# First group of a Mamba-2 kernel: GpSimd splits projection weights two pairs ahead

## Chip, cores and metric

The kernel runs on one core of a Trainium2 chip. The metric is the time on the device, in microseconds, as the median of several executions.

## The reference, cut

The input `x` is (2, 256, 512) in float32. Three blocks follow one another; the first, a Mamba-2 layer, takes nearly all of the time and is the one that the change touches.

```python
h = layernorm(x); h = rms(h) * norm_w
proj = h @ in_proj_w.T                       # gate 8192, hidden 8192, B 1024, C 1024, dt 128
hBC = silu(causal_conv(hBC, conv_w, conv_b)) # 4 taps
dt = softplus(dt + dt_bias);  A = -exp(A_log)
L = exp(segsum(A * dt))                      # decay between two positions, 0 above the diagonal
y = ((C @ B.T) * L) @ (hid * dt) + Dp * hid  # 128 heads of 64; B and C shared by 16 heads
y = y * silu(gate);  y = group_rms(y, 8 groups) * gnorm_w
x = x + (x_of_layer + y @ out_proj_w.T)
x = x + fake_quant(layernorm(x)) @ fake_quant(ctx)        # second block
x = x + ffn(layernorm(x))                                 # third block, with a small mixture
```

## The kernel before

**Tiling.** The 128 heads are worked as 64 pairs of 128 channels, all 512 tokens at once; eight pairs make a group (one group of the norm, one B and one C). Loops run over pairs: a *slot* `k` of group `g` does the front half of pair `s = 8g + k` and the back half of the pairs before it. `slots` writes the eight slots of the first group out, then a hardware loop over groups 1 to 6, then the last group. Each engine runs its own program in this slot order, and semaphores alone join them, so the order within an engine is what the code says and an instruction that waits holds up all that stand behind it on its engine.

**Precision.** Every large product is made in three passes, with each operand split into an upper part and a rest: `w_hi*h_hi + w_hi*h_lo + w_lo*h_hi`. The split of the weights is GpSimd's work. For a pair it makes `win_hi` and `win_lo` (`split_in`, `lower_in`: 128x1024, the projections to hidden and gate) from `w_raw`, and `wout_hi` and `wout_lo` (`split_out`, `lower_out`: 128x512, the output projection). `win_*` have two buffers, so the split of pair `p` may start only when TensorE has projected the gate of pair `p - 2` (semaphore `pe_gate`). `w_raw` has four buffers, filled by SyncE's queue, and a buffer is free when `lower_out` has read it (`low_wout`).

**A slot on each engine (pair s):**

- SyncE loads the weights (`w_raw`) and the rows of cumulated decay of the pair, broadcast to 128 partitions (`csx`), the latter once ScalarE is through with the pair two before (`act_exp`).
- GpSimd, for the next pair: `own_sums` (a tiny copy, `cs_own`), the split, and `select`, which fills the part above the diagonal in `csx` (two instructions). Then `sum_squares`, and the split of the output weights of this pair. In slot 4 it also splits the B and C weights of the next group (`wbc_hi`, `wbc_lo`, `lower_bc`).
- ScalarE: `decays` (8 exponentials from `csx`, and a table load before them), `tap` (first tap of the convolution, out of `ps_h`), `upper_y`, `square`, a table load, `hidden` and `gates` (two SiLUs). `decays` stands first, from slot 4 on, so all of it waits for `select`.
- VectorE: `combine` (`v`, `yg`), `scale_hidden`, `mask` (decay times C·B, 128x1536), three taps of convolution, `lower_y`.
- TensorE: hidden projection (`ps_h`), gate projection (`ps_z`), output projection of pair s - 3 (`ps_out`), the scan products of pair s - 1 (`ps_y`), and `turn`, four transposes of `hidT`, which need ScalarE's `hidden` of this slot.

TensorE, ScalarE and VectorE each have code of their own for slots 0 to 3 of the first group; GpSimd had it for slots 0 to 2. The small constants of the second block (`constants`, twelve instructions on VectorE) are made in slot 0.

Of the kernel before, what the change touches and what calls it, by code (L numbers as in the profile page):

```python
# [14 lines left out]
PPG = PAIRS // GROUPS  # L15
# [27 lines left out]
def build(nc, x_d, ctx_d, wdt_d, dtpar_d, normw_d, wmain_d, wpar_d, wbc_d, quant_d, wffn_d, ffnb_d,  # L43
# [5 lines left out]
    with ExitStack() as ctx:  # L49
# [170 lines left out]
        def _(eng):  # L220
# [15 lines left out]

            def slot(eng, s, g, k, first, last):
                r = k % 4
                if not (first and k < 4):

                    if late(s - 7):
                        eng.wait_ge(dve_ylo, s - 7)
                    eng.dma_start(par[:, k, :], wpar_d[s]).then_inc(w_in[r], 16)
                    if late(s - 3):
                        eng.wait_ge(low_wout, s - 3)
                    eng.dma_start(w_raw[:, r, :], wmain_d[s]).then_inc(w_in[r], 16)
                if first and k == 1:

                    eng.wait_ge(pre_pe, PE_TOK)
# [34 lines left out]
        def _(eng):  # L284
# [67 lines left out]
            def slot(eng, s, g, k, first, last):  # L352
# [12 lines left out]
                if first and k == 1:  # L365
                    eng.wait_ge(act_exp, 1)
                    own_sums(2, 0)
                    eng.wait_ge(w_in[3], 32)
                    eng.wait_ge(pe_gate, 2)
                    split_in(3, 1)  # L370
                    lower_in(3, 1, 4)
                    eng.wait_ge(csx_in[0], 64)
                    select(0)
                    split_out(1)
                    lower_out(1, 2)
                    return
                if first and k == 2:
                    eng.wait_ge(act_exp, 2)
                    own_sums(3, 1)
                    eng.wait_ge(csx_in[1], 64)  # L380
                    select(1)
                    split_out(2)
                    lower_out(2, 3)
                    return
                if k == 3 and not first:
                    eng.wait_ge(pe_out, s - 3)
                    eng.wait_ge(dve_ms, g)
                    eng.tensor_tensor(rstd[:], ms[:], half_neg[:], ALU.pow).then_inc(pool_rstd, 1)
# [13 lines left out]

                if not (last and k == PPG - 1):
                    split_in(n4, (k + 1) % 2)
                    if first:
                        lower_in(n4, (k + 1) % 2, s + 2)
                        eng.wait_ge(csx_in[1 - r2], 32 * (4 * g + (k + 1) // 2 + 1))
                    else:
                        eng.wait_ge(csx_in[1 - r2], 32 * (4 * g + (k + 1) // 2 + 1))
                        lower_in(n4, (k + 1) % 2, s + 2)  # L410
                    select(1 - r2)
                if k != 3 and late(s - 3):
                    eng.wait_ge(pe_out, s - 3)
# [338 lines left out]
        def _(eng):  # L752
# [87 lines left out]
            def slot(eng, s, g, k, first, last):  # L840
                if first and k == 0:
                    conv_hidden(0, 0)
                    conv_group(1, 0, ps_y, gate[:, 1, :])
                    conv_hidden(1, 1)
                    for b, bank in ((1, ps_out[:, 2, :]), (0, ps_out[:, 3, :])):
                        eng.wait_ge(pe_cb, 2 - b)
                        eng.tensor_copy(cbm[:, b, :], bank[:, 0:MJ]).then_inc(dve_cb, 1)
                    constants()
                    return
                if first and k == 1:  # L850
                    scale_hidden(1, 1)
# [10 lines left out]
                if first and k == 3:  # L862
                    combine(3, 3)
                    scale_hidden(3, 3)
                    mask(3, 0, 3)
                    lower_y(3, 3)
                    return
                combine(s, k)
                scale_hidden(s, k)
# [321 lines left out]
        def _(eng):  # L1191
# [157 lines left out]
            def project_out(s, g, k, tiles=range(TT)):  # L1349

                pair, q2, q4 = (k - 3) % PPG, (k - 3) % 2, (k - 3) % 4
                eng.wait_ge(dve_ylo, s - 2)
                for t in tiles:
                    if k == 3 and late(TT * g):
# [297 lines left out]
```

## Time and profile before

| what | us |
|---|---|
| median of 3 executions | 791.51 (788.96 to 791.81) |
| the profiled execution, its own time | 791.84 |
| its span in the profile | 789.7 |
| TensorE busy | 774.6 |
| GpSimd busy | 696.3 |
| VectorE busy | 636.4 |
| ScalarE busy | 596.5 |

The span is what the profile covers; the execution's time has about 2.1 us around it. Busy times overlap: TensorE at 98% of the span leaves some 15 us in which it does nothing, and the question for any change here is which of these stand in the stretch that it touches (the first group lies between about 20 and 120 us). Times in microseconds in the timelines are counted from the span's start.

### The profile page before, as it was taken

What the parts mean: (1) busy time and instruction counts of PE and PEld (TensorE: products, weight loads), DVE (VectorE), ACT (ScalarE), POOL (GpSimd) and SP (SyncE); (2) the same over time, 40 slices, a digit from 0 to 9 for tenths busy, and PEclk for the clock granted to TensorE, in tenths of its full rate; (3) what the DMA queues carried; (4) which work ended last, traced back from release to release, by engine and by line L of the source; (5) the groups of instructions that cost most, each with busy time, mean ns of one, the idle gap of its engine ahead of it and who ended that gap; (6) DMA issues with size and microseconds to landing.
All of it is one profiled execution on the core that took longest, in us unless ns stands there. A gap on an engine that the chain in (4) does not pass through costs nothing.

```text
span 789.7 us, 13488 instructions
## 1 busy us (share of the span) xinstructions
PE 774.6 (98%) x4275; PEld 611.2 (77%) x4275; DVE 636.4 (81%) x753; ACT 596.5 (76%) x1055; POOL 696.3 (88%) x553
## 2 busy tenths in 40 slices
PE   8989899999999999999999999999999999999997
PEld 7767677877887777877787777877787778877765
DVE  6888787888879886889779886888778778798875
ACT  5799677788778877788678877787687877788552
POOL 6689999899889998899889998999899998899551
PEclk9999999999999999999999999999999999999999
DMA  8356243344254433444243324434343333431001
GB/s 327 119 159 209 91 135 101 128 135 133 67 160 133 133 111 115 133 131 127 74 160 127 116 99 131 135 113 129 109 133 116 122 123 100 136 114 66 1 2 54
DMA packets 58028, 94.94 MB, mean 120 GB/s; under 512 B 13168, under 2 KB 46064, under 8 KB 58000
## 3 DMA queue, kind: packets, MB, share of 16 engines
q1 hardware_dynamic: 57712, 94.06, 37.6%
q10 hardware_dynamic: 288, 0.52, 0.2%
q8 instruction: 15, 0.25, 0.1%
q14 instruction: 13, 0.11, 0.0%
HBM read 93.26 MB, written 1.31 MB: 120 GB/s over the span
## 4 chain that ended last, share of the span: by engine, by line
PE 90%; POOL 4%; DVE 3%; ACT 2%; issue 1%; DMA 0%; DVEq 0%; POOLq 0%; ACTq 0%
PE ps_z L1222 25%; PE ps_out L1357 21%; PE ps_h L1222 21%; PE ps_y L1344 11%; PE ps_t L1195 4%; POOL win_lo L305 1%; PE ps_out L1195 1%; PE ps_t L1367 1%; DVE conv L814 1%; DMA acc<-in_x 0%; POOL csx L343 0%; POOL wout_lo L310 0%; POOL win_hi L296 0%; PE ps_h L1330 0%; PE ps_t L1330 0%
## 5 line engine op out<-in xcount | busy, mean ns | idle before, releaser
L305 POOL TENSOR_TENSOR win_lo<-w_raw,win_hi 128x1024 fp32r<-128x1024 f32 x64 | 182.0, 2843 | 9.7 <-DMA csx<-cs_rows 4.7
L604 ACT ACTIVATE decay<-csx,cs_own 128x256 f32<-128x256 f32 (+1 forms) x512 | 184.4, 443 | 0.8
L814 DVE SCALAR_TENSOR_TENSOR conv<-ps_h,par,conv 128x510 f32<-128x510 f32 (+2 forms) x192 | 142.9, 744 | 20.0 <-ACT conv L533 15.4
L604 ACT ACT_TABLE_LOAD x63 | 80.8, 1283 | 90.0 <-PE ps_y L1344 82.0
L899 DVE TENSOR_TENSOR decay<-decay,cbm 128x1536 f32<-128x1536 f32 x64 | 145.5, 2273 | 0.3 <-ACT decay L604 0.3
L343 POOL TENSOR_SCALAR_AFFINE_SELECT csx<-csx 128x512 f32<-128x512 f32 x128 | 109.3, 877 | 2.5 <-DMA csx<-cs_rows 2.5
L958 DVE SCALAR_TENSOR_TENSOR v<-hidT,par,ps_y 128x512 f32<-128x512 f32 x64 | 47.8, 747 | 78.3 <-PE ps_y L1344 78.2
L1357 PE MATMUL ps_out<-wout_hi,y_hi 128*128 128x512 f32 x252 | 100.3, 398 | 0.0
L1344 PE MATMUL ps_y<-decay,hid_dt 128*64 128x256 f32 (+1 forms) x1024 | 97.3, 332 | 2.4 <-DVE decay L899 1.3
L1357 PE MATMUL ps_out<-wout_lo,y_hi 128*128 128x512 f32 x252 | 99.6, 395 | 0.0
L1357 PE MATMUL ps_out<-wout_hi,y_lo 128*128 128x512 f32 x252 | 99.3, 394 | 0.0
L310 POOL TENSOR_TENSOR wout_lo<-w_raw,wout_hi 128x512 fp32r<-128x512 f32 x64 | 90.6, 1416 | 5.3
L1344 PEld LDWEIGHTS ps_y<-decay,hid_dt 128*64 128x64 f32 x1024 | 63.7, 136 | 39.5 <-issue 20.3
L967 DVE TENSOR_TENSOR yg<-v,gate 128x512 f32<-128x512 f32 x64 | 79.2, 1237 | 8.2
L436 POOL TENSOR_TENSOR sqacc<-sqacc,sq 128x512 f32<-128x512 f32 x46 | 85.5, 1859 | 0.0
L1222 PE MATMUL ps_h<-hT_hi,win_hi 128*128 128x512 f32 x256 | 74.4, 412 | 2.8 <-POOL win_lo L305 2.7
L973 DVE SCALAR_TENSOR_TENSOR y_lo<-yg,par,y_hi 128x512 fp32r<-128x512 f32 x64 | 73.1, 1141 | 0.9 <-ACT y_hi L633 0.9
L1222 PE MATMUL ps_h<-hT_lo,win_hi 128*128 128x512 f32 x256 | 69.7, 394 | 0.0
L1222 PE MATMUL ps_z<-hT_hi,win_hi 128*128 128x512 f32 x256 | 69.2, 392 | 0.0
L1222 PE MATMUL ps_z<-hT_hi,win_lo 128*128 128x512 f32 x256 | 68.8, 391 | 0.0
L1222 PE MATMUL ps_h<-hT_hi,win_lo 128*128 128x512 f32 x256 | 68.7, 390 | 0.0
L1222 PE MATMUL ps_z<-hT_lo,win_hi 128*128 128x512 f32 x256 | 68.6, 390 | 0.0
(323 smaller groups left out, 1509.6 us busy)
## 6 DMA issues: line engine op xcount, KB each, us to landing
w_raw<-in_wmain SPq DMA_DIRECT2D x64, 768.0 KB, 5.9
csx<-cs_rows SPq DMA_DIRECT2D x128, 256.0 KB, 3.5
bc_raw<-in_wbc SPq DMA_DIRECT2D x8, 517.0 KB, 5.3
ctx_raw<-in_ctx SPq DMA_DIRECT2D x1, 2048.0 KB, 14.5
par<-in_wpar SPq DMA_DIRECT2D x64, 4.0 KB, 3.6
bc_raw<-in_wffn SPq DMA_DIRECT2D x2, 512.0 KB, 4.9
out_x<-acc SPq DMA_DIRECT2D x4, 256.0 KB, 2.6
acc<-in_x ACTq DMA_DIRECT2D x2, 256.0 KB, 3.9
```

Source lines behind the costliest of these rows:

```text
L305: eng.tensor_tensor(win_lo[:, r2, :], w_raw[:, r4, 0:W_IN], win_hi[:, r2, :].bitcast(f32), ALU.subtract).then_inc(low_win, 1)
L310: eng.tensor_tensor(wout_lo[:, r4, :], w_raw[:, r4, W_IN:W_ALL], wout_hi[:, r4, :].bitcast(f32), ALU.subtract).then_inc(low_wout, 1)
L343: eng.affine_select(out=blocks[:, :, to:to + P], in_=blocks[:, :, at:at + P], compare_op=ALU.is_ge, fill=never, base=0, pattern=[[0, 2 * B ...
L436: eng.tensor_tensor(sqacc[:], sqacc[:], sq[:, n % 2, :], ALU.add).then_inc(pool_sq, 1)
L604: done = eng.activation(decay[:, r2, b, h, lo:lo + n], csx[:, r2, b, h, lo:lo + n], ACT.Exp, bias=cs_own[:, r2, t, h:h + 1])
L814: eng.scalar_tensor_tensor(out=out_b[:, :, back:], in0=src_b[:, :, 0:S - back], scalar=w[:, TAPS - 1 - back:TAPS - back], in1=out_b[:, :, ...
L899: eng.tensor_tensor(decay[:, q2], decay[:, q2], cbm[:].unsqueeze(2).broadcast_to([P, B, 2, MJ]), ALU.mult).then_inc(dve_m, 1)
L967: eng.tensor_tensor(yg[:, k % 2, :], v[:], gate[:, k % 2, :], ALU.mult).then_inc(dve_yg, 1)
L973: eng.scalar_tensor_tensor(out=y_lo[:, q2, :], in0=yg[:, q2, :], scalar=par[:, (k - 2) % PPG, 6:7], in1=y_hi[:, q2, :].bitcast(f32), op0=A ...
L1222: last = mm(out, w[:, k * P:(k + 1) * P], h[:, k, :], start=n == 0, stop=n == 3 * KT - 1)
L1344: done = mm(ps_y[h * HD:(h + 1) * HD, (b + 1) * S - n:(b + 1) * S], hid_dt[:, q2, src, h * HD:(h + 1) * HD], decay[:, q2, b, h, lo:lo + n] ...
L1357: done = mm(ps_out[:, t, :], y[:, q2, t * P:(t + 1) * P], w[:, q4, :], start=pair == 0 and n == 0, stop=pair == PPG - 1 and n == 2)
```

## The change

It touches the first group alone, but for waits. **GpSimd:** in slot 2 it also splits the weights of pair 4, and in slots 3, 4 and 5 those of pair k + 2 in place of k + 1; in slot 6 stand the B and C weights of the next group, which were in slot 4. Within slots 3 to 6 the order becomes: input split, output split, `own_sums`, `select`, `sum_squares`. Slot 7 is as it was. In slot 1 `lower_in` of pair 3 waits for VectorE's first mask (`dve_m`). **SyncE:** weights of pairs 4 to 7 are loaded one slot sooner, ahead of the `csx` rows of the slot. **VectorE:** `constants` goes from slot 0 to the end of slot 3. **TensorE:** `project_out` waits for `low_wout` of its pair in the first and last groups.

SyncE (`slot`):

```diff
                 r = k % 4
-                if not (first and k < 4):
+                if not first:
...
+                if first and 3 <= k < PPG - 1:
+
+                    eng.dma_start(par[:, k + 1, :], wpar_d[s + 1]).then_inc(w_in[(k + 1) % 4], 16)
+                    eng.wait_ge(low_wout, s - 2)
+                    eng.dma_start(w_raw[:, (k + 1) % 4, :], wmain_d[s + 1]).then_inc(w_in[(k + 1) % 4], 16)
```

GpSimd, slot 1, then slot 2, then slots 3 to 6 (`PPG` is 8, `r2` is `k % 2`, `r4` is `k % 4`):

```diff
                     split_in(3, 1)
+                    eng.wait_ge(dve_m, 1)
                     lower_in(3, 1, 4)
...
                     select(1)
+                    eng.wait_ge(w_in[0], 64)
+                    eng.wait_ge(pe_gate, 3)
+                    split_in(0, 0)
+                    lower_in(0, 0, 5)
                     split_out(2)
                     lower_out(2, 3)
                     return
-                if k == 3 and not first:
+                if first and k < PPG - 1:
+                    if k == PPG - 2:
+                        eng.wait_ge(bc_in, 16 * 2)
+                        eng.wait_ge(pe_bc, 2)
+                        eng.tensor_scalar(wbc_hi[:], bc_raw[:, 0:BC_W], 1.0, 0.0, ALU.mult, ALU.add).then_inc(hi_wbc, 1)
+                        lower_bc(2)
+                    else:
+                        eng.wait_ge(w_in[(k + 2) % 4], 32 * ((k + 2) // 4 + 1))
+                        eng.wait_ge(pe_gate, k + 1)
+                        split_in((k + 2) % 4, r2)
+                        lower_in((k + 2) % 4, r2, k + 3)
+                    if k > 3:
+                        eng.wait_ge(pe_out, k - 3)
+                    split_out(r4)
+                    lower_out(r4, k + 1)
+                    eng.wait_ge(act_exp, k)
+                    own_sums(k + 1, 1 - r2)
+                    eng.wait_ge(csx_in[1 - r2], 32 * ((k + 1) // 2 + 1))
+                    select(1 - r2)
+                    sum_squares(k, 0, k, True)
+                    return
```

VectorE (end of slot 0, then end of slot 3) and TensorE (`project_out`):

```diff
-                    constants()
                     return
...
                     lower_y(3, 3)
+                    constants()
...
                 pair, q2, q4 = (k - 3) % PPG, (k - 3) % 2, (k - 3) % 4
+                if isinstance(s, int):
+                    eng.wait_ge(low_wout, s - 2)
                 eng.wait_ge(dve_ylo, s - 2)
```

The order on GpSimd from the end of slot 2 on. Before, these were the output split of pair 2 and then slot 3, with pair 4's split and select and the output split of pair 3:

```order
L300 TENSOR_SCALAR wout_hi<-w_raw 128x512
L310 TENSOR_TENSOR wout_lo<-w_raw,wout_hi 128x512 [waits pool_wout]
L335 COPY cs_own<-cs_tok 128x8 [waits act_exp,pe_gate,w_in0]
L296 TENSOR_SCALAR win_hi<-w_raw 128x1024
L305 TENSOR_TENSOR win_lo<-w_raw,win_hi 128x1024 [waits hi_win]
L343 AFFINE_SELECT csx<-csx 128x4x128 [waits csx_in0]
L343 AFFINE_SELECT csx<-csx 128x4x128
L300 TENSOR_SCALAR wout_hi<-w_raw 128x512
L310 TENSOR_TENSOR wout_lo<-w_raw,wout_hi 128x512 [waits pool_wout]
```

Now, from the same point (after the select of pair 3):

```order
L301 TENSOR_SCALAR win_hi<-w_raw 128x1024 [waits pe_gate,w_in0]
L310 TENSOR_TENSOR win_lo<-w_raw,win_hi 128x1024 [waits hi_win]
L305 TENSOR_SCALAR wout_hi<-w_raw 128x512
L315 TENSOR_TENSOR wout_lo<-w_raw,wout_hi 128x512 [waits pool_wout]
L301 TENSOR_SCALAR win_hi<-w_raw 128x1024 [waits pe_gate,w_in1]
L310 TENSOR_TENSOR win_lo<-w_raw,win_hi 128x1024 [waits hi_win]
L305 TENSOR_SCALAR wout_hi<-w_raw 128x512
L315 TENSOR_TENSOR wout_lo<-w_raw,wout_hi 128x512 [waits pool_wout]
L340 COPY cs_own<-cs_tok 128x8 [waits act_exp]
L348 AFFINE_SELECT csx<-csx 128x4x128 [waits csx_in0]
L348 AFFINE_SELECT csx<-csx 128x4x128
```

The select of pair 4 (the last two rows) had one input split and one output split between it and the select of pair 3; now it has two of each, since pair 5's split stands there too.

On SyncE's queue, before, from the `csx` rows of pair 3 to those of pair 4:

```order
L254 DMA csx<-cs_rows 128x2x256 [waits act_exp]
L254 DMA csx<-cs_rows 128x2x256
L269 DMA bc_raw<-in_wbc 128x1034 [waits act_bc]
L243 DMA par<-in_wpar 128x8
L246 DMA w_raw<-in_wmain 128x1536 [waits low_wout]
L254 DMA csx<-cs_rows 128x2x256 [waits act_exp]
L254 DMA csx<-cs_rows 128x2x256
```

Now, from the end of slot 2 on:

```order
L249 DMA par<-in_wpar 128x8
L251 DMA w_raw<-in_wmain 128x1536 [waits low_wout]
L259 DMA csx<-cs_rows 128x2x256 [waits act_exp]
L259 DMA csx<-cs_rows 128x2x256
L274 DMA bc_raw<-in_wbc 128x1034 [waits act_bc]
L249 DMA par<-in_wpar 128x8
L251 DMA w_raw<-in_wmain 128x1536 [waits low_wout]
L259 DMA csx<-cs_rows 128x2x256 [waits act_exp]
L259 DMA csx<-cs_rows 128x2x256
```

Pair 4's weights (the first two rows now) are issued ahead of the `csx` rows of pair 3, and pair 5's where pair 4's were.

## Rows read from the trace of the kernel before

**Rows 1.** The page, part 1: the engines' busy time over the span.

```profile
PE 774.6 (98%) x4275; PEld 611.2 (77%) x4275; DVE 636.4 (81%) x753; ACT 596.5 (76%) x1055; POOL 696.3 (88%) x553
```

**Rows 2.** Waits of TensorE over the whole span: total us, times, longest.

```profile
PE ps_h L1222 <- POOL win_lo L305: 2.7, 1, 2.7
...
PE ps_y L1344 <- DVE decay L899: 1.3, 1, 1.3
...
PE ps_y L1344 <- issue: 1.1, 1, 1.1
```

**Rows 3.** Windows: length, busy us of PE, PEld, DVE, ACT, POOL, PEclk, DMA share, GB/s.

```profile
50.00:60.00 10.00, 8.84 (x49) 6.73 (x48) 9.18 (x9) 9.93 (x19) 9.03 (x8) 1.00 0.64 189
...
80.00:90.00 10.00, 7.62 (x26) 6.13 (x27) 6.59 (x5) 5.97 (x13) 9.83 (x9) 0.83 0.07 27
```

**Rows 4.** Timeline of TensorE, first group: start us, us, engine, line, operation, [idle].

```profile
58.79 1.20 PE L1222 MATMUL ps_h<-hT_hi,win_hi 128*128 128x512 f32 x4
...
68.73 0.66 PE L1195 MATMUL ps_t<-ident,hidT 128*128 128x128 f32 x4
69.14 1.17 PE L1222 MATMUL ps_h<-hT_hi,win_hi 128*128 128x512 f32 x4
...
71.97 1.07 PE L1222 MATMUL ps_z<-hT_hi,win_hi 128*128 128x512 f32 x4
...
79.04 0.66 PE L1195 MATMUL ps_t<-ident,hidT 128*128 128x128 f32 x4
...
82.38 1.88 PE L1222 MATMUL ps_h<-hT_hi,win_hi 128*128 128x512 f32 x4 [2.68 <-POOL win_lo L305]
...
86.82 1.09 PE L1222 MATMUL ps_z<-hT_hi,win_hi 128*128 128x512 f32 x4
...
93.91 0.66 PE L1195 MATMUL ps_t<-ident,hidT 128*128 128x128 f32 x4
```

**Rows 5.** Timeline of GpSimd, first group.

```profile
49.31 1.22 POOL L343 TENSOR_SCALAR_AFFINE_SELECT csx<-csx 128x512 f32<-128x512 f32 x2 [1.61 <-DMA csx<-cs_rows]
...
54.99 3.74 POOL L305 TENSOR_TENSOR win_lo<-w_raw,win_hi 128x1024 fp32r<-128x1024 f32 x1
...
58.70 1.67 POOL L343 TENSOR_SCALAR_AFFINE_SELECT csx<-csx 128x512 f32<-128x512 f32 x2
```

**Rows 6.** Timeline of ScalarE, first group.

```profile
58.93 5.65 ACT L604 ACTIVATE decay<-csx,cs_own 128x256 f32<-128x256 f32 x16
...
67.70 0.63 ACT L612 ACTIVATE hidT<-conv 128x512 f32<-128x512 f32 x1
...
84.02 1.28 ACT L604 ACT_TABLE_LOAD   x1 [5.97 <-POOL csx L343]
...
92.02 0.63 ACT L612 ACTIVATE hidT<-conv 128x512 f32<-128x512 f32 x1
```

**Rows 7.** Groups of GpSimd by line, 0 to 200 us: busy us, mean ns, idle.

```profile
L305 POOL TENSOR_TENSOR win_lo<-w_raw,win_hi 128x1024 fp32r<-128x1024 f32 x18 | 50.7, 2817 | 1.9 <-DMA csx<-cs_rows 0.5
L343 POOL TENSOR_SCALAR_AFFINE_SELECT csx<-csx 128x512 f32<-128x512 f32 x34 | 27.4, 828 | 2.5 <-DMA csx<-cs_rows 2.5
L310 POOL TENSOR_TENSOR wout_lo<-w_raw,wout_hi 128x512 fp32r<-128x512 f32 x16 | 26.1, 1629 | 1.3
L296 POOL TENSOR_SCALAR win_hi<-w_raw 128x1024 fp32r<-128x1024 f32 x17 | 17.8, 1049 | 0.0
...
L300 POOL TENSOR_SCALAR wout_hi<-w_raw 128x512 fp32r<-128x512 f32 x16 | 13.6, 851 | 0.0
...
L335 POOL COPY cs_own<-cs_tok 128x8 f32<-128x8 f32 (+1 forms) x18 | 8.4, 464 | 8.0 <-ACT cs_tok L549 5.3 <-ACT decay L604 1.5 <-issue 1.2
```

**Rows 8.** Instructions by tile, 30 to 200 us: ns minimum/median/maximum, first and last start.

```profile
L305 POOL TENSOR_TENSOR win_lo<-w_raw,win_hi x16: 2339/2560/4412, 33.6 to 198.5; 128x1024 fp32r<-128x1024 f32 x16
...
L310 POOL TENSOR_TENSOR wout_lo<-w_raw,wout_hi x15: 1277/1296/2860, 44.7 to 196.0; 128x512 fp32r<-128x512 f32 x15
...
L300 POOL TENSOR_SCALAR wout_hi<-w_raw x15: 612/623/2116, 43.6 to 194.9; 128x512 fp32r<-128x512 f32 x15
```

More of the change, by code:

```diff
@@ L384, in slot @@
                     return
-                if k == 3 and not first:
+                if first and k < PPG - 1:
[19 more added lines that the diff above has]
+                    return
+                if k == 3:
                     eng.wait_ge(pe_out, s - 3)
@@ L404, in slot @@
                     split_in(n4, (k + 1) % 2)
[L405 to L410, printed above, removed]
+                    eng.wait_ge(csx_in[1 - r2], 32 * (4 * g + (k + 1) // 2 + 1))
+                    lower_in(n4, (k + 1) % 2, s + 2)
                     select(1 - r2)
```

## Prediction

> **What bounds the kernel now.** I read the page first: TensorE is busy 774.6 of 789.7 us [rows 1]. The waits of TensorE tell where the rest is. Nothing of over half a microsecond stands after the first group, so what TensorE gains or loses there goes into the end one for one. In the stretch of the change it waits three times: 1.3 us for a mask of VectorE, 1.1 us ahead of the third scan, and 2.7 us for the `win_lo` of pair 6 [rows 2]. The window around the last wait has a mean granted clock of 0.83, that around the wait of 1.1 us has 1.00 [rows 3]: only the long wait is followed by matmuls at the lower of the two levels (1.2 instead of 2.4 GHz). From the start of `ps_h` to that of `ps_z` slot 6 takes 86.82 - 82.38 = 4.44 us and slot 5 takes 71.97 - 69.14 = 2.83 [rows 4]: 1.6 us more. The transposes ended at 79.45 (79.04, and 0.41 from one `turn` to the next matmul [rows 4]), so the place costs 2.9 + 1.6 = 4.5 us.
>
> Then the timelines of GpSimd and ScalarE, to see who is late at that place. GpSimd has no idle time there, and in the same stretch ScalarE waits 5.97 us for the `select` of pair 6 [rows 6]. So both things that GpSimd makes, split weights and selected rows, were late, and a change of their order can only move lateness from one to the other unless it saves time on GpSimd.
>
> **The early part.** Without `constants` between the copies and the first mask the 1.3 us wait goes. GpSimd, though, is held by the `csx` rows of pair 3, which are loaded when ScalarE has finished a pair that hangs on nothing moved here, and land at 49.31 [rows 5]; I leave that time as it is. The new wait on `dve_m` stands before this and is hidden by the 1.61 us of idle time at 49.31 [rows 5]: if the cover is gone it costs what `lower_in` is late, 1.6 us at most. Behind 49.31 VectorE's mask product and a `win_lo` are at work together, and the `win_lo` takes 3.74 us [rows 5] against a minimum of 2.34 [rows 8]. It will still be so, and the third scan waits for that mask. Between 0 and the 1.3 + 1.1 of both waits I take 0.9 us of gain at the start of slot 4: 57.9 in place of 58.79 [rows 4]. SyncE's earlier loads cost nothing: pair 4's go out while that queue waits for ScalarE anyway; if they did not, `csx` of pair 3 would be late, which is the start of the next part. The moved `constants` (some 2 us) lie in slot 3, where the mask has a whole slot until its scan. The waits on `low_wout` are for splits two slots old: nothing.
>
> **Slot 4: the select of pair 4.** Between the selects of pair 3 and pair 4 GpSimd now has two full sets of splits. By the means of its groups [rows 7] a set is `win_hi` 1.05, `win_lo` 2.82, `wout_hi` 0.85, `wout_lo` 1.63: 6.35 us; a select is 2 x 0.83 = 1.66 and `own_sums` 0.46. The select of pair 4 ends at 49.31 + 1.66 + 12.7 + 0.46 + 1.66 = 65.8. Before, it ended at 58.70 + 1.67 = 60.4 [rows 5]. What is queued behind it: ScalarE's `decays(4)`, and behind that on the same engine `tap`, `upper_y`, `square`, a table load and `hidden(4)`, for which TensorE's `turn` waits. Sixteen exponentials took 5.65 us [rows 6], so eight take 2.83: 68.6. From the end of the exponentials (64.58) to the start of `hidden` (67.70) were 3.12 us, and `hidden` takes 0.63 [rows 6]: `turn` of slot 4 starts at 72.4. TensorE would be ready at 57.9 + (68.73 - 58.79) = 67.8 [rows 4]. So a wait of 4.6 us arises, longer than the 2.68 that was followed by the low clock, and I charge the same 1.6 us after it. `turn(4)` is 3.6 us later than before.
>
> **Slots 5 and 6.** Slot 5 starts at 72.8; with 4.44 to `ps_z` and 2.83 for that, `ps_z(5)` ends at 80.0. Its `turn` comes 79.04 - 71.97 = 7.07 after the start of `ps_z` [rows 4], at 84.3, and slot 6 starts at 84.7. The old wait for `win_lo` is gone. `ps_z(6)` starts at 87.5 (before: 86.82) and `turn(6)` is due 7.09 later, at 94.6. But GpSimd may split pair 7 only after `ps_z(5)` (`pe_gate`), and the select of pair 6 now stands behind this split: 80.0 + 6.35 + 0.46 + 1.66 = 88.5. ScalarE took 92.02 - 84.02 = 8.0 us from the end of that wait to `hidden(6)`, and 0.63 for it [rows 6]: `turn(6)` at 97.1, against 93.91 [rows 4]. **Sum: +3.2 us.** It passes through to the end, as later slots have slack: the B and C split ends at about 88.5 + 1.9 + 3.5 = 93.9, before TensorE wants it, and from slot 7 on GpSimd is ahead of where it was.
>
> The profiled execution was 791.84, so +3.2 is 795.0; the median of the runs shown lies 0.3 lower, which makes **794.7 us**.
>
> **Bounds of the one uncertain price,** how much GpSimd loses to VectorE. With the minima [rows 8] a set is 1.05 + 2.34 + 0.61 + 1.28 = 5.28, a select 1.22 [rows 5]. The select of pair 4 then ends at 62.8, `turn(4)` starts at 69.4 after a wait of 1.6, near the waits of 1.3 and 1.1, of which the latter left the clock at 1.00 [rows 3], so without the 1.6. `ps_z(5)` ends at 75.5, the select of pair 6 at 82.4, and `turn(6)` comes at 91.1: -2.8 us. With a `win_lo` of 3.74, as at 54.99 [rows 5], a set is 7.3: select at 67.7, `turn(4)` at 74.3, `ps_z(5)` end at 82.0, `turn(6)` at 100.0: +6.1 us. I take the means, since both engines do the same work per slot in the new stretch as over the 200 us of the means.
>
> A rule of the Trainium skill bears on this. The page "SBUF — State Buffer", section "Who interferes with whom", says that a VectorE instruction with two inputs in SBUF shuts out a GpSimd instruction that reads SBUF, for the whole of whichever comes first. By that rule each mask should hold up GpSimd in full, which is the case of +6.1 us. The rows agree in single cases (3.74 instead of 2.34), while the mean of 2.82 says that it meets them in part only.
>
> **Rivals.**
> *Few collisions* (GpSimd near its minima): -2.8 to about +1 us, 789 to 792.5. For it: the order is new, and the wait on `dve_m` keeps one pair apart. Chance 0.22.
> *More loss:* the wait of 2.5 us at `turn(6)` (97.1 - 94.6) is near the 2.68 that brought the low clock; a second time at 1.6 us makes +4.8, and the heavy collisions +6.1: 796.3 to 797.6. Chance 0.30.
> *The gain comes whole:* the waits of 1.3, 1.1 and 2.9 and the slow 1.6 go and nothing replaces them: -6.9 us, 784.6. It needs the select of pair 4 by about 61 and that of pair 6 before `ps_z(5)` has left GpSimd time for a split; only if ScalarE's chain had slack that I miss. Chance 0.06.
> *Nothing happens:* the split of pair 6 is still what TensorE waits for. It would have to be 10 us later than in my walk. Chance 0.02.
> The forecast itself, +1 to +4 us (792.5 to 795.5), has 0.40.
>
> **Numbers.** A measurement of this kernel tells about 0.5%, 4 us, from no change. Slower by more: the 0.30 and a little of the forecast, 0.33. Faster by more: 0.07. Between: 0.60. The range goes from the case of the minima (-2.8) to that of heavy collisions (+6.1): 788.5 to 797.6.
>
> **What would show it.** In the profile after: no wait of `ps_h` for `win_lo` at slot 6; a new one of TensorE's transposes of `hidT` at 67 to 73 us with a lower clock behind it, and a second at about 95; ScalarE waiting for `csx` of GpSimd ahead of the exponentials of slots 4 and 6; the first scan 1.3 us earlier. The prediction is wrong if the select of pair 4 ends before 62 or after 68 us, if GpSimd does not wait for TensorE ahead of pair 7's split, or if a wait appears beyond slot 7.

## Result, and the profile after

| | before | after |
|---|---|---|
| median of the undisturbed executions | 791.41 us (4 runs, 788.96 to 791.81) | 799.54 us (4 runs, 798.93 to 799.61) |
| span of the profiled execution | 789.7 us | 797.6 us |
| ratio of after to before | | 1.0102, 95% interval 1.008 to 1.0124 |

The change makes the kernel 1.0% slower. The forecast was 794.7 us with a range up to 797.6, and slower by over 0.5% had a chance of 0.33. The place and the chain were as forecast; the loss was 7.9 us of span in place of 3.2, because TensorE's low clock cost 4.0 us where 1.6 had been charged, and the two late selects were later than the walk had them.

The page of the changed kernel, part 1. TensorE's busy time rises by 1.9 us from [rows 1] with the same matmuls, and the other 6.0 of the 7.9 us are idle time of TensorE:

```profile
PE 776.5 (97%) x4275; PEld 613.2 (77%) x4275; DVE 636.2 (80%) x753; ACT 596.6 (75%) x1055; POOL 692.7 (87%) x553
```

The waits of TensorE over the whole span (us in total, times, longest). The wait for `win_lo` and that for the mask of [rows 2] are gone; the transposes now wait twice for ScalarE's `hidT`, 9.1 us in all, and the wait ahead of the third scan has grown from 1.1 to 1.9. That is 11.0 us in place of 5.1, nearly all of the 6.0:

```profile
PE ps_t L1222 <- ACT hidT L639: 9.1, 2, 5.6
...
PE ps_y L1371 <- issue: 1.9, 1, 1.9
```

The timeline of TensorE in the first group, to be laid beside [rows 4]:

```profile
57.46 0.66 PE L1222 MATMUL ps_t<-ident,hidT 128*128 128x128 f32 x4
57.87 1.17 PE L1249 MATMUL ps_h<-hT_hi,win_hi 128*128 128x512 f32 x4
...
66.44 1.52 PE L1371 MATMUL ps_y<-decay,hid_dt 128*64 128x256 f32 x16
73.58 1.12 PE L1222 MATMUL ps_t<-ident,hidT 128*128 128x128 f32 x4 [5.62 <-ACT hidT L639]
74.35 2.05 PE L1249 MATMUL ps_h<-hT_hi,win_hi 128*128 128x512 f32 x4
...
79.50 1.09 PE L1249 MATMUL ps_z<-hT_hi,win_hi 128*128 128x512 f32 x4
...
86.61 0.66 PE L1222 MATMUL ps_t<-ident,hidT 128*128 128x128 f32 x4
87.02 1.17 PE L1249 MATMUL ps_h<-hT_hi,win_hi 128*128 128x512 f32 x4
...
100.42 1.12 PE L1222 MATMUL ps_t<-ident,hidT 128*128 128x128 f32 x4 [3.44 <-ACT hidT L639]
101.19 2.06 PE L1249 MATMUL ps_z<-hT_hi,wbc_hi 128*128 128x512 f32 x4
...
104.99 1.08 PE L1249 MATMUL ps_h<-hT_hi,win_hi 128*128 128x512 f32 x4
```

Slot 4 starts at 57.87, 0.92 us sooner than before. Then the two waits come, at slots 4 and 6. Behind each the same four transposes take 1.12 instead of 0.66, and the four first matmuls some 2.05 instead of 1.17: the low clock. The windows say so too (columns as in [rows 3]; the third figure from the end is the granted clock):

```profile
70.00:80.00 10.00, 6.42 (x19) 5.21 (x20) 7.34 (x8) 8.46 (x16) 5.13 (x7) 0.66 0.20 65
80.00:90.00 10.00, 10.00 (x56) 7.82 (x55) 6.74 (x8) 4.01 (x6) 7.24 (x7) 1.00 0.38 121
...
100.00:110.00 10.00, 9.57 (x38) 7.95 (x39) 9.76 (x10) 7.85 (x16) 9.85 (x9) 0.84 0.50 144
```

Why ScalarE's `hidT` is late is seen on GpSimd (beside [rows 5]). Two whole sets of splits stand between the selects at 48.81 and 64.08, the latter takes 2.75 us for its two instructions, and behind its work of slot 4 the engine stands still for 7.38 us ahead of the split of pair 7, with the select of pair 6 (88.93) queued behind that split:

```profile
48.81 1.22 POOL L348 TENSOR_SCALAR_AFFINE_SELECT csx<-csx 128x512 f32<-128x512 f32 x2 [1.58 <-DMA csx<-cs_rows]
...
51.57 2.72 POOL L310 TENSOR_TENSOR win_lo<-w_raw,win_hi 128x1024 fp32r<-128x1024 f32 x1
54.25 2.13 POOL L305 TENSOR_SCALAR wout_hi<-w_raw 128x512 fp32r<-128x512 f32 x1
...
64.08 2.75 POOL L348 TENSOR_SCALAR_AFFINE_SELECT csx<-csx 128x512 f32<-128x512 f32 x2
...
82.60 1.05 POOL L301 TENSOR_SCALAR win_hi<-w_raw 128x1024 fp32r<-128x1024 f32 x1 [7.38 <-PE ps_z L1249]
...
88.93 2.75 POOL L348 TENSOR_SCALAR_AFFINE_SELECT csx<-csx 128x512 f32<-128x512 f32 x2
```

And ScalarE (beside [rows 6]). Both its long waits end with a select: the one put down to `issue` ends at 66.92, 0.1 us after the select of pair 4, which ended at 64.08 + 2.75 = 66.83:

```profile
66.92 2.87 ACT L631 ACTIVATE decay<-csx,cs_own 128x256 f32<-128x256 f32 x8 [6.49 <-issue]
...
72.90 0.63 ACT L639 ACTIVATE hidT<-conv 128x512 f32<-128x512 f32 x1
...
91.75 1.28 ACT L631 ACT_TABLE_LOAD   x1 [7.71 <-POOL csx L348]
...
99.74 0.63 ACT L639 ACTIVATE hidT<-conv 128x512 f32<-128x512 f32 x1
```

### The profile page after: what moved, and what is told of

It reads as the page before. It is cut to its first block, busy times and chain, and to the rows that moved or that the text cites. A ratio compares the mean times of both kernels' runs of the same rounds, so it can differ in the third digit from the quotient of the medians.

```text
span 797.6 us, 13506 instructions
## 1 busy us (share of the span) xinstructions
PE 776.5 (97%) x4275; PEld 613.2 (77%) x4275; DVE 636.2 (80%) x753; ACT 596.6 (75%) x1055; POOL 692.7 (87%) x553
## 4 chain that ended last, share of the span: by engine, by line
PE 88%; POOL 6%; ACT 1%; DVE 1%; issue 1%; DMA 1%; DVEq 0%; SPq 0%; POOLq 0%; ACTq 0%
PE ps_z L1249 25%; PE ps_out L1386 21%; PE ps_h L1249 20%; PE ps_y L1371 11%; PE ps_t L1222 4%; POOL win_lo L310 2%; POOL csx L348 1%; POOL wout_lo L315 1%; POOL win_hi L301 1%; PE ps_out L1222 1%; PE ps_t L1396 1%; POOL wout_hi L305 1%; DMA csx<-cs_rows 0%; POOL cs_own L340 0%; DMA acc<-in_x 0%
## 5 line engine op out<-in xcount | busy, mean ns | idle before, releaser
L841 DVE SCALAR_TENSOR_TENSOR conv<-ps_h,par,conv 128x510 f32<-128x510 f32 (+2 forms) x192 | 142.9, 744 | 26.7 <-ACT conv L560 22.1
L348 POOL TENSOR_SCALAR_AFFINE_SELECT csx<-csx 128x512 f32<-128x512 f32 x128 | 111.3, 892 | 2.5 <-DMA csx<-cs_rows 2.5
L315 POOL TENSOR_TENSOR wout_lo<-w_raw,wout_hi 128x512 fp32r<-128x512 f32 x64 | 86.8, 1356 | 5.3
L301 POOL TENSOR_SCALAR win_hi<-w_raw 128x1024 fp32r<-128x1024 f32 x63 | 66.5, 1055 | 7.4 <-PE ps_z L1249 7.4
L1000 DVE SCALAR_TENSOR_TENSOR y_lo<-yg,par,y_hi 128x512 fp32r<-128x512 f32 x64 | 70.9, 1107 | 0.2 <-ACT y_hi L660 0.2
```

Of the source, the lines that this page charges most:

```text
L301: eng.tensor_scalar(win_hi[:, r2, :], w_raw[:, r4, 0:W_IN], 1.0, 0.0, ALU.mult, ALU.add).then_inc(hi_win, 1)
L315: eng.tensor_tensor(wout_lo[:, r4, :], w_raw[:, r4, W_IN:W_ALL], wout_hi[:, r4, :].bitcast(f32), ALU.subtract).then_inc(low_wout, 1)
L348: eng.affine_select(out=blocks[:, :, to:to + P], in_=blocks[:, :, at:at + P], compare_op=ALU.is_ge, fill=never, base=0, pattern=[[0, 2 * B ...
L841: eng.scalar_tensor_tensor(out=out_b[:, :, back:], in0=src_b[:, :, 0:S - back], scalar=w[:, TAPS - 1 - back:TAPS - back], in1=out_b[:, :, ...
```

## Experiments

Each is the changed kernel or the one before with one thing altered, or with two where the text says so. Ratios are to the kernel before, timed beside them on the same chip, so one less than 1 is faster than before. The medians of the kernel before were 791.42 us beside experiments 1 to 4, 790.83 beside 5 to 8 and 791.37 beside 9 to 11, and its executions spread from 788.9 to 795.9 us; a ratio is not exactly the quotient of two medians, and both carry an uncertainty of about 0.2%. I held three theories apart. A: the selects are late because they stand behind two sets of splits, and behind a split that waits for TensorE. B: the moved `constants` or collisions of VectorE and GpSimd make them late. C: GpSimd has no time left in the first group, so that any order is late somewhere.

In timelines the first transposes of a kernel differ by about 0.7 us between executions (see the last section), so I compare distances within the group where this matters. The traces of experiments 1 to 6, 8, 10 and 11 have the early start, those of the kernel before and of the changed kernel the late one.

### 1. Selects first in slots 3 to 6

```diff
 if first and k < PPG - 1:
+    eng.wait_ge(act_exp, k)
+    own_sums(k + 1, 1 - r2)
+    eng.wait_ge(csx_in[1 - r2], 32 * ((k + 1) // 2 + 1))
+    select(1 - r2)
     if k == PPG - 2:
...
-    eng.wait_ge(act_exp, k)
-    own_sums(k + 1, 1 - r2)
-    eng.wait_ge(csx_in[1 - r2], 32 * ((k + 1) // 2 + 1))
-    select(1 - r2)
     sum_squares(k, 0, k, True)
```

> The changed kernel with one edit: in slots 3 to 6 of the first group GpSimd does own_sums and select ahead of the splits, everything else stays (splits two pairs ahead, B and C weights in slot 6, earlier loads, constants in slot 3). Theory A (the selects stand behind splits, and the one of pair 6 behind a split that waits for TensorE): both waits of the transposes for hidT, 5.6 and 3.4 us, and the low clock behind them go. Select of pair 4 ends near 60 us, transposes of slot 4 start near 67.9, of slot 6 near 88.5 (before 93.91, changed kernel 100.42): about 5 us faster than before, ratio 0.993 to 0.995. Theory B (GpSimd simply loses more time to VectorE in the first group, whatever its order): slot 6 still waits, for select or for a split, and the kernel stays slower than before, 1.003 to 1.010.

Measured: 791.50 us, ratio 0.9992 (0.9973 to 1.0012). The 8 us of the change are gone, so the place of the selects is what cost them. The gain that I expected beyond that did not come. TensorE's timeline:

```profile
55.31 2.27 PE L1377 MATMUL ps_y<-decay,hid_dt 128*64 128x256 f32 x16 [1.90 <-issue]
...
68.66 0.66 PE L1228 MATMUL ps_t<-ident,hidT 128*128 128x128 f32 x4
...
90.51 0.66 PE L1228 MATMUL ps_t<-ident,hidT 128*128 128x128 f32 x4 [0.82 <-ACT hidT L645]
...
92.64 1.39 PE L1255 MATMUL ps_z<-hT_hi,wbc_hi 128*128 128x512 f32 x4 [1.48 <-POOL wbc_lo L320]
```

The transposes of slot 6 come at 90.51, 3.4 us sooner than in [rows 4], 0.8 of it from the early start. But then TensorE waits 1.48 us for the B and C weights, and the low clock follows: the granted clock of 90 to 100 us is 0.83, and what takes 3.3 us at full speed from the transposes to `ps_h` of pair 7 (90.51 to 97.08) takes 6.6 with the wait. GpSimd has no idle time between 48 and 104 us. This is theory C, on top of A. It is not all that was missing: in this trace the low clock came behind the wait of the third scan too, 2.27 us for the first row where the changed kernel takes 1.52, and from there to `ps_z` of slot 4 it cost 1.6 us.

### 2 and 3. Select first in slot 3 alone, and in slot 5 alone

```diff
+    if k == 3:
+        eng.wait_ge(act_exp, k)
+        own_sums(k + 1, 1 - r2)
+        eng.wait_ge(csx_in[1 - r2], 32 * ((k + 1) // 2 + 1))
+        select(1 - r2)
     if k == PPG - 2:
...
-    eng.wait_ge(act_exp, k)
-    own_sums(k + 1, 1 - r2)
...
+    if not (k == 3):
+        eng.wait_ge(act_exp, k)
+        own_sums(k + 1, 1 - r2)
...
```

Experiment 3 is the same with `k == 5`.

> The changed kernel with own_sums and select ahead of the splits in slot 3 only. Theory A: the wait of 5.6 us at the transposes of slot 4 goes with the low clock behind it; slot 5 is as in the changed kernel, where the select of pair 6 stands behind the split of pair 7, which waits for the gate projection of pair 5, so a wait of about 3 us at the transposes of slot 6 stays, with some 1.3 us of low clock. Transposes of slot 6 near 91.5 us; end about 1 us earlier than before, ratio 0.997 to 1.001. Theory B: no gain of more than 2 us over the changed kernel, ratio 1.007 or more.

> The changed kernel with own_sums and select ahead of the splits in slot 5 only. Theory A: the transposes of slot 4 still wait 5.6 us, those of slot 6 start when they are due, near 97.0 us, and keep the full clock: 3.4 + 1.3 = 4.7 us less than the changed kernel, about 3.2 us slower than before, ratio 1.003 to 1.005. GpSimd's idle time ahead of the split of pair 7 stays but nothing waits behind it. If the two waits are one delay that only shows twice, slot 6 gains nothing: ratio 1.010.

Measured: slot 3 alone 794.25 us, ratio 1.0027 (1.0007 to 1.0047); slot 5 alone 794.75 us, 1.0027 (1.0007 to 1.0047). TensorE with the select first in slot 3 alone:

```profile
67.86 0.66 PE L1228 MATMUL ps_t<-ident,hidT 128*128 128x128 f32 x4 [0.79 <-ACT hidT L645]
...
83.36 1.12 PE L1228 MATMUL ps_t<-ident,hidT 128*128 128x128 f32 x4 [5.12 <-ACT hidT L645]
...
96.23 0.66 PE L1228 MATMUL ps_t<-ident,hidT 128*128 128x128 f32 x4
```

and in slot 5 alone:

```profile
72.97 1.11 PE L1228 MATMUL ps_t<-ident,hidT 128*128 128x128 f32 x4 [5.62 <-ACT hidT L645]
...
95.61 0.66 PE L1228 MATMUL ps_t<-ident,hidT 128*128 128x128 f32 x4
```

The second is as expected: the wait of 3.44 at slot 6 is gone with its low clock, and the kernel is 4.8 us faster than the changed one (4.7 expected). In the first I missed the place. The wait of slot 4 shrinks to 0.79, but one of 5.12 comes at slot 5, where I had expected one of about 3 at slot 6: the select of pair 4 now stands ahead of slot 3's splits and that of pair 5 behind slot 4's, so that the two sets lie between these two. Either edit alone takes some 5 us off the changed kernel. Undoing the first late select moves the wait to slot 5; the one of slot 6 is gone there, since `ps_z` of pair 5 is no longer late and GpSimd does not wait for it.

### 4. The clock kept up during the waits

```diff
+                if first and k in (4, 6):
+                    for _ in range(85 if k == 4 else 50):
+                        mm(ps_t[:, 0:P], onesb[:], onesb[:], start=True, stop=True)
                 turn(s, r2)
```

These are extra matmuls whose result nobody reads.

> The changed kernel with 85 and 50 extra small matmuls (128x128, bf16, into ps_t, which the transposes then overwrite) ahead of the transposes of slots 4 and 6 of the first group, so that TensorE is at work through the waits. If the low clock behind the waits is a cost of its own: slot 5's hidden projection takes 2.83 us instead of 5.15 and the transposes 0.41 instead of 0.77, which makes 2.7 us, and slot 6 gives 1.3: about 4 us less than the changed kernel, 3.9 slower than before, ratio 1.004 to 1.006. If the filling delays the transposes, or the clock drops all the same: ratio 1.009 to 1.012.

Measured: 795.89 us, ratio 1.0043 (1.0024 to 1.0062). The median is 3.65 us below that of the changed kernel, with the same late selects.

```profile
68.31 6.29 PE L1314 MATMUL ps_t<-onesb 128*128 128x128 bf16 x85
74.44 0.60 PE L1222 MATMUL ps_t<-ident,hidT 128*128 128x128 f32 x4
74.81 1.17 PE L1249 MATMUL ps_h<-hT_hi,win_hi 128*128 128x512 f32 x4
```

`ps_h` of slot 5 is at full speed (1.17 for its first four, where the changed kernel has 2.05). The medians also hold what happens elsewhere, so I go by the traces: from the transposes of slot 4 to `ps_h` of slot 8 TensorE takes 41.0 us here and 44.5 in the changed kernel, 3.5 less, with 2.7 of gain in slot 5 and 1.1 in slot 6. The transposes of slot 4 start 0.7 us after `hidT` is ready (73.74), as the extra matmuls still run, so a part is lost again. So some 3.5 us of the changed kernel's time are the low clock behind its two waits; the late selects make both the waits and this.

### 5. The kernel before, with the B and C split one slot later

```diff
-                if k == 4:
+                if k == (5 if first else 4):
                     eng.wait_ge(bc_in, 16 * (g + 2))
...
-                if k == 4:
+                if k == (5 if first else 4):
                     eng.tensor_scalar(wbc_hi[:], bc_raw[:, 0:BC_W], 1.0, 0.0, ALU.mult, ALU.add).then_inc(hi_wbc, 1)
```

> The kernel before with one edit: in the first group GpSimd splits the B and C weights at the end of slot 5 instead of slot 4 (loop and last group as before). Theory A (what costs is which piece stands ahead of the one that TensorE or ScalarE waits for): split and select of pair 6 come 3.5 us earlier, so the wait of 2.7 us for win_lo and the low clock behind it go, 4.5 us, and the B and C weights are ready at about 88.7 us, before they are wanted at 89.8: ratio 0.994 to 0.996. Theory C (GpSimd has no time to spare in the first group, so a moved piece is missed at its new place): the wait comes back at the B and C projection or at the hidden projection of pair 7, and the gain is under 2.5 us: ratio 0.997 to 1.000.

Measured: 791.98 us, ratio 1.0015 (1.0 to 1.0029). The wait of [rows 2] for `win_lo` is gone and the transposes of slot 6 come at 88.60, 5.3 us sooner than in [rows 4] (0.8 of it from the early start). Nearly all is given back one slot later, where the select of pair 7 is late and with it, through ScalarE, VectorE's convolution of B and C:

```profile
88.60 0.66 PE L1195 MATMUL ps_t<-ident,hidT 128*128 128x128 f32 x4
...
101.46 1.16 PE L1222 MATMUL ps_z<-hT_hi,win_hi 128*128 128x512 f32 x4 [3.16 <-DVE conv_bc L814]
```

So a piece of 3.4 us of GpSimd's work can be moved, and the lateness moves with it: theory C for the kernel before.

### 6. The same, with `constants` in slot 3 and the wait on `dve_m`

```diff
                         eng.tensor_copy(cbm[:, b, :], bank[:, 0:MJ]).then_inc(dve_cb, 1)
-                    constants()
...
                     lower_y(3, 3)
+                    constants()
...
                     split_in(3, 1)
+                    eng.wait_ge(dve_m, 1)
                     lower_in(3, 1, 4)
```

> As the previous kernel, and also the constants at the end of VectorE's slot 3 and the wait on dve_m, as in the change: the parts of the change that reorder nothing on GpSimd within a slot. Theory A: 1.3 us more than the previous kernel, 5.5 to 5.8 us faster than before, ratio 0.992 to 0.994. Theory C: GpSimd ends slot 5 at about the same time, and the early 1.3 us is waited away later: ratio as the previous kernel within 0.001.

Measured: 790.63 us, ratio 0.9991 (0.9975 to 1.0007). TensorE now waits for `win_lo` of pair 4:

```profile
58.61 1.61 PE L1223 MATMUL ps_h<-hT_hi,win_hi 128*128 128x512 f32 x4 [1.76 <-POOL win_lo L305]
60.01 1.91 PE L1223 MATMUL ps_h<-hT_lo,win_hi 128*128 128x512 f32 x4
```

An early gain of VectorE finds GpSimd late at the next place, at the low clock. The measured time can't be told from that of the kernel before. It is 1.4 us below that of experiment 5, more than the 0.001 that theory C allowed, but the two intervals meet.

### 7. The changed kernel with `constants` back in slot 0

> The changed kernel with the constants back in VectorE's slot 0. The first scan waits for the mask again, 1.3 us. In slot 3 the constants took 5.3 us of VectorE's time in the changed kernel, 56.8 to 62.2, since they met GpSimd's splits; without them v, yg and the mask of pair 4 come earlier, and fewer collisions fall on the select of pair 4. If the late select of pair 4 (66.8 us against 65.8 in the forecast) is due to these collisions, it ends 1 to 2 us earlier and the kernel is equal to the changed one or up to 1.5 us faster, ratio 1.007 to 1.010. If they do not matter, it ends where it did, at 66.8, and so does the kernel, ratio 1.010.

Edit: the two lines of the diff on VectorE undone. Measured: 799.27 us, ratio 1.01 (1.0084 to 1.0116), the same as the changed kernel. In the latter `constants` had taken 5.3 us of VectorE (56.84 to 62.15 us, the costliest rows below), and the mask of slot 4 (that of pair 3) ended just ahead of its scan. VectorE's rows there, with the masks of slots 4 and 6:

```profile
56.84 1.29 DVE L936 CAST identb<-ident 128x128 bf16<-128x128 f32 x1
...
59.33 2.31 DVE L947 CAST onesr<-onesf 1x128 fp32r<-1x128 f32 x1
...
64.60 1.74 DVE L926 TENSOR_TENSOR decay<-decay,cbm 128x1536 f32<-128x1536 f32 x1
...
89.45 1.74 DVE L926 TENSOR_TENSOR decay<-decay,cbm 128x1536 f32<-128x1536 f32 x1
```

With them back in slot 0 (VectorE's mask, then GpSimd's select of pair 4):

```profile
61.21 2.69 DVE L926 TENSOR_TENSOR decay<-decay,cbm 128x1536 f32<-128x1536 f32 x1 [0.58 <-ACT decay L631]
```

```profile
65.84 1.22 POOL L348 TENSOR_SCALAR_AFFINE_SELECT csx<-csx 128x512 f32<-128x512 f32 x2
```

The two selects of pair 4 lay behind the mask and took 1.22 us instead of 2.75, but they began at 65.84 and ended at 67.06 (66.83 in the changed kernel). Theory B falls for `constants`, and experiment 1, where VectorE and GpSimd still meet, shows that collisions alone do not make the 8 us: they are there, and what was saved on one instruction here was lost on another. The trace is that of the slowest execution (801.29 us, the others 798.8 to 799.5); in it the low clock behind the wait at slot 6 cost 2.7 us.

### 8. A third buffer for the split of pair 7

```diff
-        win_hi = sb("win_hi", [P, 2, W_IN], f32r)
+        win_hi = sb("win_hi", [P, 3, W_IN], f32r)
...
-                        eng.wait_ge(pe_gate, k + 1)
-                        split_in((k + 2) % 4, r2)
+                        if k < 5:
+                            eng.wait_ge(pe_gate, k + 1)
+                        split_in((k + 2) % 4, 2 if k == 5 else r2)
```

The same for `win_lo`, and TensorE reads pair 7's weights there. The order on every engine is that of the changed kernel.

> The changed kernel with a third buffer of win_hi and win_lo, used for pair 7 alone, so that its split in GpSimd's slot 5 does not wait for the gate projection of pair 5; the order of instructions is that of the changed kernel. Theory A (the select of pair 6 is late because it stands behind a split that waits for TensorE): GpSimd's 7.4 us of idle time goes, the select ends near 83 us, the transposes of slot 6 start when due, near 97 us, at full clock: 4.7 us less than the changed kernel, ratio 1.003 to 1.005. Rival (the two splits and collisions alone make it late, the wait for TensorE only fills the time): the wait at the transposes of slot 6 stays above 2 us, ratio above 1.007.

Measured: 793.56 us, ratio 1.0034 (1.0022 to 1.0046), 6.0 us less than the changed kernel where I expected 4.7. From the transposes of slot 5 to `ps_h` of slot 8 the trace shows the 4.7: 26.7 us against 31.5. Another 1.1 lies ahead of them, where the low clock behind the wait of slot 4 happened to be cheaper. GpSimd goes straight on:

```profile
73.56 1.27 POOL L460 TENSOR_TENSOR sqacc<-sq 128x512 f32<-128x512 f32 x1
74.81 1.49 POOL L301 TENSOR_SCALAR win_hi<-w_raw 128x1024 fp32r<-128x1024 f32 x1
...
82.68 1.22 POOL L348 TENSOR_SCALAR_AFFINE_SELECT csx<-csx 128x512 f32<-128x512 f32 x2
```

The select of pair 6 begins 6.2 us sooner with the same work ahead of it, and slot 6 has no wait. What made it late was the split's wait for TensorE ahead of it on the same engine.

### 9, 10 and 11. ScalarE makes the upper part of the B and C weights

If GpSimd is the bound (theory C), then taking work off it should gain what no order did. In 9 (on version 1) and 10 (on the kernel before) `wbc_hi` is made by ScalarE:

```diff
                 upper_y(s, k)
+                if first and k == 6:
+                    eng.wait_ge(bc_in, 16 * 2)
+                    eng.wait_ge(pe_bc, 2)
+                    eng.activation(wbc_hi[:], bc_raw[:, 0:BC_W], ACT.Copy).then_inc(hi_wbc, 1)
                 square(s, g, k, first)
...
                 gates(s, k)
+                if first and k == 4:
+                    eng.wait_ge(bc_in, 16 * 2)
...
```

The first piece is that of 9, the second that of 10, with the same three lines. GpSimd's own instruction for it is left out in the first group. Version 11 is 5 with the second piece at `k == 5`.

> The kernel with selects first in slots 3 to 6, in which ScalarE makes the upper part of the B and C weights of slot 6, in the idle time that it has there ahead of the square (1.97 us for sqacc). GpSimd as the bound: it is rid of 1.21 us between the select of pair 6 and wbc_lo, so TensorE's wait of 1.48 us for wbc_lo falls to about 0.3, and with the low clock behind it (two groups of 1.9 and 1.7 us instead of about 1.1) gone, 2.5 us are gained against the version with selects first: 789, ratio 0.996 to 0.998. Rival, ScalarE is the bound as well (it is behind by what its new 1 us instruction takes): turn of slot 6 is 1 us later and the ratio stays at 0.999 to 1.0.

> The kernel before, in which ScalarE makes the upper part of the next group's B and C weights behind the gates of slot 4, where it waits 0.8 us for the select of pair 5 anyway; order and places of all else as before. GpSimd as the bound: the win_lo of pair 6 comes 1.05 us sooner, TensorE's wait of 2.68 us falls to 1.6, perhaps without the low clock behind it: 1.1 to 2.7 us, ratio 0.9965 to 0.9985. Rival, the wait hangs on something else than GpSimd's load: no change.

> The kernel before with the B and C split in slot 5 and its upper part made by ScalarE behind the gates of slot 5, where it waits 5.58 us for the select of pair 7. GpSimd as the bound: the select of pair 7 comes 1.05 us sooner, the wait of 3.16 us for conv_bc falls to about 2.1, so 1 to 2 us less than the version with the split merely moved: ratio 0.9975 to 0.999. Rival, slot 7 hangs on something else: ratio 1.001 as with the move alone.

Measured, with the kernel before at 791.37 us beside them: 9 is 789.45 us, ratio 0.9965 (0.9947 to 0.9982); 10 is 788.92 us, 0.9964 (0.9945 to 0.9982); 11 is 790.35 us, 0.9982 (0.996 to 1.0003). Version 9, TensorE:

```profile
91.11 0.66 PE L1231 MATMUL ps_t<-ident,hidT 128*128 128x128 f32 x4 [0.77 <-ACT hidT L644]
92.07 1.20 PE L1258 MATMUL ps_z<-hT_hi,wbc_hi 128*128 128x512 f32 x4 [0.30 <-POOL wbc_lo L320]
```

Version 10, TensorE, then ScalarE's new instruction:

```profile
78.30 0.66 PE L1200 MATMUL ps_t<-ident,hidT 128*128 128x128 f32 x4
80.53 1.20 PE L1227 MATMUL ps_h<-hT_hi,win_hi 128*128 128x512 f32 x4 [1.58 <-POOL win_lo L305]
```

```profile
67.98 1.05 ACT L597 ACTIVATE wbc_hi<-bc_raw 128x1024 fp32r<-128x1024 f32 x1
```

Both came out as expected. In 9 the wait for `wbc_lo` falls from 1.48 to 0.30 and no low clock follows. In 10 that for `win_lo` falls from 2.68 to 1.58, the first matmuls behind it take 1.20 instead of 1.88, and the transposes of slot 6 come 12.55 us after those of slot 5 (78.30 to 90.85), against 14.87 in [rows 4]. One instruction of 1.05 us, moved to an engine with idle time, gains about 2.5 us (0.9964, with an interval that means 1.4 to 4.4 us). Versions 9 and 10 can't be told apart by their times, and both beat both kernels. In 11 the select of pair 7 began 1.05 us sooner (91.33 against 92.38 in version 5) and the wait for `conv_bc` ended 1.04 sooner, as expected; in the profiled execution the low clock followed this wait (2.01 us for the first four matmuls of `ps_z`, 1.16 in version 5) and took it back, so the two spans are equal. The medians are 1.6 us apart, with intervals that meet.

## Why the prediction was wrong

The range ended at 797.6 and the time was 799.54. The mechanism held; terms of the sum were too small. The largest is the low clock, charged with 1.6 us once, where it cost 2.7 us at slot 4 and 1.3 at slot 6: 2.4 of the 4.7 us that were missed. The late selects and the hand-overs behind them make the rest. By the steps of the prediction:

- **The early part: right, with some luck in the size.** Slot 4 starts at 57.87, forecast 57.9. The first mask is no longer waited for; the third scan still waits, 1.87 us, so the waits give 0.5 us. Another 0.3 came from a gap that the prediction did not look at: from the transposes to `ps_h` of slot 4 are 0.41 us (57.46 to 57.87), and 0.72 before. No row shows the wait on `dve_m` to decide.
- **`constants` in slot 3 cost nothing: right for the end, not for its working.** They took 5.3 us, not some 2, and the mask of slot 4 had no slack left (64.60 + 1.74 = 66.34, scan at 66.44). Experiment 7 shows that nothing else hung on it.
- **Slot 4, the place and the chain: right, 1.2 us short.** The select of pair 4 ended at 66.83, not 65.8. From the select of pair 3 to that of pair 4 were 64.08 - 48.81 = 15.3 us, forecast 14.8. The first set ran beside a mask of 3.37 us and took 7.9 us busy (1.49, 2.72, 2.13, 1.59), the second 5.4, near the minima of [rows 8]; together 0.6 above twice the mean. The select's 2.75 instead of the mean of 1.66 was the dearer part, 1.1 us, and the earlier start of pair 3's gave 0.5 back. The turn of slot 4 came at 73.58, forecast 72.4.
- **The charge for the low clock: mis-sized, the first step that failed.** I had charged 1.6 us, what it cost behind a wait of 2.68 [rows 4]. Behind a wait of 5.62 it lasted through all of `ps_h`: 79.50 - 74.35 = 5.15 us against 2.83, and 0.77 instead of 0.41 from `turn` to `ps_h`. That is 2.7 us. It is not what a wait of this length always costs: experiment 3 has the same wait, and there it was 2.0. `turn(5)` is 2.3 us later than forecast, 1.2 of it from the select and 1.1 from this.
- **Slot 6, the wait of GpSimd for `ps_z(5)`: right in mechanism.** It waited 7.38 us there, and experiment 8 shows that this wait, ahead of the select on the same engine, is what makes the select of pair 6 late. From its end to the select's end were 91.68 - 82.60 = 9.1 us, forecast 8.5: again a select of 2.75. So `turn(6)` came at 100.42 instead of 97.1. Every delay of `ps_z(5)` goes into it one for one, which is why the errors of slot 4 did not stay there.
- **The second low clock: priced, but as a rival.** It came, and cost 104.99 - 100.42 = 4.57 against 97.20 - 93.91 = 3.29 us before, 1.3 us.
- **The sum and the range.** From 3.2: + 1.2 for slot 4's select, + 1.1 for the longer low clock, + 1.0 for slot 6 (0.6 its split and select, the rest in hand-overs), + 1.3 for the second low clock: 7.8, measured 7.9. The range ended at the walk with heavy collisions, +6.1. In that walk too `turn(6)` comes at 100.0 and is due at 96.6, a wait of 3.4 us and longer than the 2.68 that brought the low clock, yet a second low clock (+1.6) stood beside it as an alternative. Added, the two would have reached 799.2, still 0.3 short: the select of pair 4 came sooner than in the heavy walk (66.8 against 67.7), but the low clock behind it was dearer.
- **Collisions.** The prediction weighed a rule of the Trainium skill, page "SBUF — State Buffer", section "Who interferes with whom", by which a VectorE instruction with two SBUF inputs shuts a GpSimd instruction out. The trace agrees for what overlaps: the selects of pairs 4 and 6, begun 0.5 us ahead of a mask of 1.74 (64.60 and 89.45), took 2.75 us both, and 1.22 where no mask ran (experiments 7 and 8). It holds for no whole chain, since a mask meets one or two of GpSimd's instructions in a slot: one set took 7.9, above even the 7.3 of the prediction's heavy case, the next 5.4. In sum the means came nearest.
- **After slot 7: right.** No wait appears beyond it, and `ps_h` of slot 8 is 7.8 us late, as the end is. The reading that nothing of over half a microsecond stands after the first group overlooked a wait of 1.17 us of TensorE at 764.21 (771.90 now); it stays the same and absorbed nothing.

What I had not seen is why the kernel before waited 2.7 us at all. The prediction said that both of GpSimd's products were late there and that an order only moves lateness; it did not ask how much time GpSimd lacked. Experiments 1, 5 and 6 gave three other orders within 0.2% of the kernel before, each with a wait for GpSimd's work, direct or by way of ScalarE, somewhere else, and 9 and 10 gained with 1.05 us taken off the engine. So GpSimd's time between 48 and 104 us is the bound that these runs show; the change spent 7.4 us of it on waiting.

Open: the change's wait on `low_wout` and the earlier loads were not tried alone; no row shows them to cost, and experiment 1 has them and is as fast as the kernel before. Why the executions of one kernel differ by up to 7 us (the kernel before, granted clock 0.995 to 1.000 over the whole) was not looked into; the low clock that follows a wait in one execution and not in another may be a part. An order without idle time and with `wbc_hi` on ScalarE (version 9) did not beat the order of the kernel before with the same edit (10), so whether any order of the changed kernel's kind is worth keeping is not shown.

## What to carry to other kernels

If two products of one engine are both late, look for a piece to take off it before reordering it: here 1.05 us moved to an engine with idle time gained about 2.5 us, while no order tried without that gained. An instruction that feeds a chain (the select) must not stand behind one that waits for the engine at the chain's end. When one mechanism brings on another, as a long wait does the low clock behind it, add their prices in each case of the range; don't hold them as alternatives.

## What the runs showed of the hardware

**The low clock behind a wait.** Which waits of TensorE of 1.4 us and more were followed by the lower of its two levels (1.2 instead of 2.4 GHz), in the profiled executions of the first group, with the experiment in brackets: none after 1.58 (10), 1.87 (the changed kernel), 1.88 (9), 1.90 (3), 1.95 (2), 2.00 (7) and 3.16 us (5); the low clock after 1.48 (1), 1.76 (6), 1.90 (1), 2.16 (4), 2.39 (8), 2.68 (before), 2.75 (11), 3.44 (the changed kernel), 3.46 (7) and all from 4.14 to 5.62. So between 1.5 and 3.2 us the length of the wait alone does not decide. Nor does it set the price, which I take as the time of the stretch behind the wait beyond what the same stretch takes at full speed: 1.5 to 1.7 us behind waits of 1.48, 1.76, 1.90, 2.39, 2.68, 2.75 and 4.14 us, 1.3 behind 3.44, 2.7 behind 3.46, 2.5 to 2.6 behind 5.07 (7) and 5.12 (2), and behind 5.62 once 2.7 (the changed kernel) and once 2.0 (3). All that cost over 1.7 lie behind waits of over 3.4 us.

**Filler matmuls keep the clock up.** 85 small matmuls in the wait and 50 in the other gave back some 3.5 us (experiment 4). Behind its wait of 2.16 us the clock was low at first (0.91 over 60 to 80 us; 74 ns for one of the 85, 59 for one of the 50), and full behind them (1.17 for the next `ps_h`).

**GpSimd beside VectorE.** For the same shape, the two selects of a pair took 1.22 to 2.75 us (most often 1.22, 1.67 or 2.75), `wout_hi` 0.61 to 2.13, and VectorE's mask 1.74 to 3.37. VectorE's cast of one row of 128 numbers took 2.31 us beside GpSimd's `win_lo` of 59.17 to 61.57, and 0.83 in experiment 4, where the `win_lo` began as it ended.

**The start.** Before the first group, executions fall into two kinds 0.7 us apart: the transposes of slot 0 at 32.6 us (before, after, 7, 9) or at 31.8 to 31.9 (the others), with a granted clock of 0.91 or 1.00 over the first 20 us. A comparison of two single traces carries this 0.7 us with it.
